# A transformer sandwich kernel: the first fillers read a constant, the last layer's scale row moves to ScalarE, and the tiles are laid out anew

## The reference, cut to what matters

```
x = x + layernorm(attention(layernorm(x)))          # 8 batches x 256 tokens x 128; softmax over 256 keys
h = silu(lin(z, w1)) * lin(z, w2)                   # z = layernorm(x); 128 -> 512
h = gelu(lin(h, h1)); h = gelu(lin(h, h2))          # 512 -> 512, exact gelu
x = x + layernorm(lin(h, w3))                       # 512 -> 128
# lin(z, w) = (z @ w.T) * s, with one scale s per output column; all in fp32
```

## Time and profile before

| what | us |
|---|---|
| time, median of 3 runs (lowest to highest) | 132.6 (132.56 to 133.0) |
| the profiled execution, its time | 133.0 |
| the profiled execution, its span from first to last instruction | 131.1 |
| PE busy in the span | 123.2 (94%) |
| DVE / ACT / POOL busy | 101.5 / 97.2 / 28.5 |

### The profile page before, as it was taken

The page is one execution under the profiler, slowest core; times in us unless marked ns, Lnnn a source line. Parts: engine busy times, 40 slices in busy tenths (PEclk is TensorE's granted clock), DMA queues, the critical chain, the costliest instruction groups (busy, mean ns, idle before and its releaser), DMA issues.

```text
span 131.1 us, 2357 instructions
## 1 busy us (share of the span) xinstructions
PE 123.2 (94%) x699; PEld 102.0 (78%) x699; DVE 101.5 (77%) x339; ACT 97.2 (74%) x180; POOL 28.5 (22%) x41
## 2 busy tenths in 40 slices
PE   5999999999899999999999999999999999999950
PEld 4677869888778888887889888888787887799940
DVE  1587898998799989838799898376989935996660
ACT  3238887986999748399999095999993996996510
POOL 5282420035300054002000463300021330000450
PEclk9999999999999999999999999999999999999999
DMA  4799996001200000000000001020000011000021
GB/s 111 246 342 387 376 388 218 1 5 14 69 0 5 0 7 0 0 0 0 5 0 0 0 5 40 0 80 10 0 0 0 0 52 33 0 5 0 5 80 43
DMA packets 5344, 8.28 MB, mean 63 GB/s; under 512 B 464, under 2 KB 2768, under 8 KB 5328
## 3 DMA queue, kind: packets, MB, share of 16 engines
q1 hardware_dynamic: 3984, 5.19, 12.0%
q0 software_dynamic: 1344, 2.88, 6.8%
HBM read 7.02 MB, written 1.05 MB: 62 GB/s over the span
## 4 chain that ended last, share of the span: by engine, by line
PE 85%; DVE 6%; DMA 2%; issue 1%; ACT 1%; POOL 1%; SPq 0%; DVEq 0%; ACTq 0%
PE F L1170 22%; PE F L1176 22%; PE F L1123 5%; PE A L1051 5%; PE F L1130 5%; PE A L1083 4%; PE A L1170 2%; PE A L1176 2%; PE A L1034 2%; PE A L1067 2%; DMA wa_raw<-w_attn 2%; PE A L1022 2%; PE A L1014 1%; PE F L1199 1%; PE A L1211 1%
## 5 line engine op out<-in xcount | busy, mean ns | idle before, releaser
L317 POOL TENSOR_TENSOR rstd<-mv,minus_half 128x4 f32<-128x4 f32 (+1 forms) x19 | 18.4, 971 | 89.3 <-DVE mv L619 89.3
L1170 PE MATMUL F<-a_hi,h_hi 128*128 128x512 f32 (+1 forms) x160 | 37.5, 356 | 0.0
L1176 PE MATMUL F<-a_lo,h_hi 128*128 128x512 f32 (+1 forms) x160 | 36.8, 350 | 0.2 <-DVE a_lo L612 0.2
L612 DVE TENSOR_TENSOR a_lo<-act_full,a_hi 128x512 fp32r<-128x512 f32 (+1 forms) x52 | 30.1, 601 | 5.2 <-ACT act_full L430 4.9
L438 ACT ACTIVATE a_hi<-F,sc 128x512 fp32r<-128x512 f32 (+1 forms) x35 | 21.1, 627 | 14.1 <-PE F L1176 13.9
L1176 PEld LDWEIGHTS F<-a_lo,h_hi 128*128 128x128 f32 x160 | 26.6, 188 | 5.1 <-DVE a_lo L612 0.8
L1170 PEld LDWEIGHTS F<-a_hi,h_hi 128*128 128x128 f32 x160 | 25.9, 188 | 4.2 <-ACT act_full L430 0.4
L430 ACT ACTIVATE act_full<-F,sc 128x512 f32<-128x512 f32 (+1 forms) x40 | 23.4, 619 | 1.6 <-PE F L1176 1.6
L715 DVE SCALAR_TENSOR_TENSOR act_full<-F,sc,silu 128x512 f32<-128x512 f32 (+1 forms) x16 | 10.7, 676 | 1.9 <-ACT silu L419 1.6
L1123 PE MATMUL F<-x2T_hi,w_hi 128*128 128x512 f32 (+1 forms) x32 | 10.3, 404 | 0.5 <-issue 0.3
L419 ACT ACTIVATE silu<-F,sc 128x512 f32<-128x512 f32 (+1 forms) x16 | 9.9, 634 | 1.0 <-PE F L1130 0.7
(11 more groups left out here) (154 smaller groups left out, 194.5 us busy)
## 6 DMA issues: line engine op xcount, KB each, us to landing
h_raw<-h SPq DMA_DIRECT2D x2, 1024.0 KB, 11.2
h_hi<-h POOLq DMA_DIRECT2D x2, 1024.0 KB, 9.2
xs<-x SPq DMA_DIRECT2D x3, 256.0 KB, 3.9
out<-outs SPq DMA_DIRECT2D x3, 256.0 KB, 2.2
w_raw<-w SPq DMA_DIRECT2D x1, 512.0 KB, 6.4
w_hi<-w POOLq DMA_DIRECT2D x1, 512.0 KB, 7.0
xs<-x SPq DMA_DIRECT2D x2, 128.0 KB, 8.7
w_raw<-w SPq DMA_DIRECT2D x1, 256.0 KB, 15.5
```

Source lines behind the costliest of these rows:

```text
L317: nc.gpsimd.tensor_tensor(rstd[:, ln, tiles(b)], mv[:, ln, tiles(b), 1], minus_half[:, 0:SIZES[b]], ALU.pow).then_inc(rstd_ready[ln], 1)
L612: nc.vector.tensor_tensor(dst, full, hi.bitcast(f32), ALU.subtract).then_inc(done, 1)
L1170: nc.tensor.matmul(out, terms[k][0], terms[k][2], start=(k == 0), stop=False)
L1176: last = [nc.tensor.matmul(out, terms[k][0], terms[k][3], start=False, stop=(k == KT - 1)) for out, terms in groups]
```

## The change

The fillers read a constant of the preamble, one bf16 value per partition, spread over 256 columns, instead of the tile `warm`; the clearing of `warm`, its semaphore and PE's wait for it are gone. The first groups of fillers become 13, 3 and 2 where they were 10, 6 and 3; the eight later ones stay. `w3_diagonal` and `w3_row_copy` move from DVE to ACT, where each is an activation of the kind Copy, between `xT_copy(0)` and `gT_copy(0)`, and between `v_copy(0)` and `exps(0, 0)`. The allocation has a new order: after `wa_raw` come three small tiles of together 384 bytes, then all the tiles whose size is a multiple of 2048 bytes, then the rest.

```diff
         wa_raw = sb("wa_raw", [P, 3 * D])
+        rstd = sb("rstd", [P, 4, TILES])
+        neg_max = sb("neg_max", [P, TILES])
+        sums = sb("sums", [P, TILES])
+
+        x2T_hi, x2T_lo = sb("x2T_hi", [P, TOK], f32r), sb("x2T_lo", [P, TOK], f32r)
+        a_hi = [sb(f"a{n}_hi", [P, KT, TOK], f32r) for n in (1, 2, 3)]
+        a_lo = [sb(f"a{n}_lo", [P, KT, TOK], f32r) for n in (1, 2, 3)]
+        act_full = sb("act_full", [P, KT, TOK])
+        silu1 = sb("silu1", [P, 2, TOK])
         w12_hi = sb("w12_hi", [P, 2 * HID], f32r)
...
-        sc = sb("sc", [P, N_SCALES])
-        qk = sb("qk", [P, D])
...
-        warm = sb("warm", [P, 512], mybir.dt.bfloat16)
...
+        warm = nc.const_aps.tensor(1.0, [P, 2 * P], mybir.dt.bfloat16)
+        qk = sb("qk", [P, D])
...
+        sc = sb("sc", [P, N_SCALES])
...
         @block.gpsimd
         def _(pool):
-            nc.gpsimd.memset(warm[:, :], 0.0).then_inc(warm_ready, 1)
             nc.gpsimd.memset(ident[:, :], 0.0).then_inc(zeroed, 1)
...
+            def w3_diagonal():
+                act.wait_ge(sc_loaded, 16)
+                act.wait_ge(ident_ready, 1)
+                nc.scalar.activation(w3_diag[:, :], ident[:, :], ACT.Copy, scale=sc[:, S_W3:S_W3 + 1]).then_inc(w3_diag_ready, 1)
+
+            def w3_row_copy():
+                act.wait_ge(w3_row_in_psum, 1)
+                nc.scalar.activation(w3_row[:, :], A[3][:, 0:D], ACT.Copy).then_inc(w3_row_ready, 1)
+
             qk_copy()
             xT_copy(0)
+            w3_diagonal()
             gT_copy(0)
             v_copy(0)
+            w3_row_copy()
             exps(0, 0)
...
-            def w3_diagonal():
-                dve.wait_ge(sc_loaded, 16)
-                dve.wait_ge(ident_ready, 1)
-                nc.vector.tensor_scalar(w3_diag[:, :], ident[:, :], sc[:, S_W3:S_W3 + 1], None, ALU.mult).then_inc(w3_diag_ready, 1)
-
-            def w3_row_copy():
-                dve.wait_ge(w3_row_in_psum, 1)
-                nc.vector.tensor_copy(w3_row[:, :], A[3][:, 0:D]).then_inc(w3_row_ready, 1)
-
             x_statistics(0)
             x_normalised(0)
-            w3_diagonal()
             x_statistics(1)
...
             squared_sums(0)
-            w3_row_copy()
             pT_copy(0, 0)
...
-                    nc.tensor.matmul(bank[:, 0:256], warm[:, 0:P], warm[:, 0:256], start=True, stop=True)
+                    nc.tensor.matmul(bank[:, 0:256], warm[:, 0:P], warm[:, :], start=True, stop=True)
...
-            pe.wait_ge(warm_ready, 1)
-            keep_warm(A[0], 10)
+            keep_warm(A[0], 13)
             qk_product()
             pe.wait_ge(ident_ready, 1)
-            keep_warm(A[0], 6)
+            keep_warm(A[0], 3)
             x_transposes(0)
-            keep_warm(A[0], 3)
+            keep_warm(A[0], 2)
             g_projection(0)
```

More of the change, by code:

```diff
@@ L60, in sem @@
             return ctx.enter_context(nc.semaphore(name))
+        LN_X, LN_O, LN_X1, LN_Y = range(4)
+        LOW_PARTS = ((0, 3), (3, 6))
         wa_raw = sb("wa_raw", [P, 3 * D])
+        rstd = sb("rstd", [P, 4, TILES])
[6 more added lines that the diff above has]
+        silu1 = sb("silu1", [P, 2, TOK])
         w12_hi = sb("w12_hi", [P, 2 * HID], f32r)
@@ L69, in sandwich_kernel @@
         w3_raw = sb("w3_raw", [P, KT * D])
-        sc = sb("sc", [P, N_SCALES])
-        qk = sb("qk", [P, D])
[L72 to L75, removed]
-        warm = sb("warm", [P, 512], mybir.dt.bfloat16)
[L77 to L80, removed]
         w3_scaled = sb("w3_scaled", [P, KT * D])
-        flags = sb("flags", [1, 2])
-        LOW_PARTS = ((0, 3), (3, 6))
         xs = sb("xs", [P, TILES, D])
@@ L90, in sandwich_kernel @@
         y_n = sb("y_n", [P, TB, D])
[L91 to L106, removed]
         yT = sb("yT", [P, TOK])
+        low_bits = sb("low_bits", [P, 2 * HID], mybir.dt.bfloat16)
         F = [bank(f"F{i}") for i in range(4)]
@@ L124, in sandwich_kernel @@
         borrowed, odd, even = Lane(), attention_buffers("odd"), attention_buffers("even")
+        low_pairs = sb("low_pairs", [P, HID], mybir.dt.bfloat16)
+        warm = nc.const_aps.tensor(1.0, [P, 2 * P], mybir.dt.bfloat16)
+        qk = sb("qk", [P, D])
+        wv = wa_raw[:, 2 * D:3 * D]
+        ident = sb("ident", [P, P])
+        ones_sq, w3_diag, w3_row = sb("ones_sq", [P, P]), sb("w3_diag", [P, D]), sb("w3_row", [P, D])
+        stats = sb("stats", [P, 4, TILES, 9])
+        mv = sb("mv", [P, 4, TILES, 2])
+        o_shift = sb("o_shift", [P, TILES])
+        y_scaled = sb("y_scaled", [P, TILES])
+        y_shift = sb("y_shift", [P, TILES])
+        sc = sb("sc", [P, N_SCALES])
+        minus_half = sb("minus_half", [P, TB])
+        ones = sb("ones", [P, 1])
+        low_sums = sb("low_sums", [P, 6])
+        flags = sb("flags", [1, 2])
         borrowed.xn = act_full[:, 1, 0:half].rearrange("p (t d) -> p t d", d=D)
@@ L160, in sandwich_kernel @@
             sem("w12_rounded"), sem("h1_rounded"), sem("h2_rounded"), sem("w3_rounded"))
-        warm_ready = sem("warm_ready")
         zeroed, ident_ready, eps_ready = sem("zeroed"), sem("ident_ready"), sem("eps_ready")
```

## The result

The changed kernel takes 131.61 us (median of 6 runs, 131.16 to 131.82), the kernel before 132.58 (median of 6 runs beside it, 132.18 to 134.55): a ratio of 0.989, interval 0.9851 to 0.9928. By these medians it is faster by 1.0 us, the small end of that interval; on two other chips it was 2.0 and 1.6 us (e9, e15). The prediction had 132.3 and took "the same" for the likeliest. The range held the time, but the step on which the prediction rested is only the first of three gains.

What follows compares the result with a forecast made beforehand. PE was taken as the bound: busy 94% of the span, 85% of the chain. Only six fillers becoming three counted, 0.25 us off the 132.6 median, all else 0: about 132.3 us, range 131.5 to 133.8.

Steps and rivals of the forecast that it cites:

- "the same": Outcome class for the whole kernel: no change beyond the 0.3% a measurement can tell; chance 0.47.
- the step on which the prediction rested: Cutting six fillers to three ahead of block 0's transposes; 0.25 us, the whole forecast gain.
- Constant instead of `warm`: PE's start: begins 0.57 us earlier, thirteen fillers end at 3.50, before the qk product's data; POOL's lost work worth 0.
- Six fillers become three: Before block 0's transposes: ACT's copy of xT up to 0.31 us earlier, by the clock's rise; 0.25 taken.
- Three fillers become two: Between transposes and g projection, which waits for ACT's copy and not the fillers; worth 0 on the path.
- `w3_row_copy` on ACT: In ACT's idle time before the exponentials; shortens DVE's work ahead of the `attend(0, 0)` copy, 0 to 0.1 us, 0 taken.
- `w3_diagonal` on ACT: Between ACT's copies of xT and g, covered by 0.1 us; DVE's freed time and earlier POOL loads worth 0.
- New addresses: Large tiles at multiples of 2048: float32r streaming could gain or lose up to 5.7 us; 0 taken.
- The small gains add up: Rival: transposes 0.31, copy ahead of `attend(0, 0)` 0.1, earlier loads up to 0.2; 131.6 to 132.2 us, chance 0.14.
- The addresses speed up float32r: Rival: 32-byte phase causes float32r's 7.5% excess, so half to all of 5.7 us goes; 127 to 130, chance 0.11.
- Nothing on the path: Rival: with an early clock rise the six fillers never stood in the way; 132.5 to 132.7 us, chance 0.12.
- The clock comes up late: Slower rival: fewer early fillers delay PE's clock, transposes to scores cost up to 2.05 us more; 133.0 to 134.5, chance 0.15.

Runs made afterwards that it cites:

- e9: The changed kernel as it is, run again on another chip: 131.42 us, ratio 0.985 to the kernel before.
- e15: The changed kernel as it is, run a third time on a further chip: 131.4 us, ratio 0.9869 to the kernel before.
- e3: The kernel before with only the constant in the fillers and the counts 13, 3, 2; old addresses, scale row on DVE: 132.55 us, ratio 0.9966.
- e7: The changed kernel with the float32r weights alone 32 bytes further on, activations left in place: 134.08 us in one execution.
- e10: The changed kernel with the old counts of the later fillers (13, 6, 3): 131.65 us, ratio 0.9868 to the kernel before.
- e14: The kernel before with filler counts 10, 3, 2, still waiting for `warm`: 132.81 us, ratio 0.9974.
- e11: The changed kernel with the float32r weights alone 64 bytes further on: 133.39 us in one execution.
- e4: The kernel before with only the scale row's two steps moved from DVE to ACT: 132.5 us, ratio 0.9952.
- e5: The changed kernel with seven added waits at the head of DVE's list, bringing it back to 448 records: 132.32 us, ratio 0.9925 to the kernel before.
- e6: The kernel before with the scale row's two steps on ACT and seven added waits at the head of DVE's list: 133.14 us, ratio 0.9991.
- e1: The changed kernel with the tiles in the old allocation order, every tile at its old address: 131.69 us, ratio 0.9887 to the kernel before.
- e8: The changed kernel with all float32r tiles, weights and activations alike, 32 bytes further on: 131.41 us in one execution.
- e2: The kernel before with the new allocation order of tiles alone: 132.77 us, ratio 0.9969.

## Why the prediction was right or wrong

**Constant instead of `warm`**: right. Thirteen fillers fit (the last starts at 3.29, the qk product at 3.69) at the price of the old ones, 0.21 us apart, and no row shows anybody waiting for POOL's lost operation. What it does to the rise of the clock the prediction counts with the next step: it took the same 3.9 us behind the first filler, so 4.6 us. That is not a fixed distance. In the three traces of the changed kernel it shifts from one execution to the next: by the spacing of the matmuls it was about 4.3 us in the first, between 5.6 and 6.1 in e9, and between 5.8 and 6.3 in e15. Over all traces it goes from 3.7 (e3) to 9.9 us (e7). The GHz that the prediction gives for the two levels are in no view; the rows show the spacings of fillers of 256 columns, 0.21 and 0.11 us.

**Six fillers become three**: right in place, 0.25 taken, 0.48 measured in the profile of the whole start, of which 0.37 lie between x and the copy. The 0.31 of the working was for transposes at the high clock; the clock rose earlier still than the 4.6 us assumed, and x came 0.11 us earlier. That the 0.48 came out so well is partly luck: against the same trace before, e9 and e15 gain 0.19 and 0.01. The steadier figure is e3's 0.45 by the times, for the constant and the counts together; that the counts do it isn't shown (e10, e14). The mean of the maxima's start is 8.33 in ten traces that start PE at 0.78, and 8.80 in five that start it at 1.32; this leaves out e7 and e11, and with their late clocks the ten become twelve with a mean of 8.62.

**Three fillers become two**, **`w3_row_copy` on ACT**: right for the path, no row shows anything of them on it. `w3_row_copy` has left DVE's list too, though, and so has its part in the next step.

**`w3_diagonal` on ACT**: right on its place and its cover (done at 6.02, load at 6.11, so 0.09 us to spare where 0.1 was forecast), and no row shows a cost of the earlier POOL loads. It is wrong in the sentence on DVE, "so this is worth 0". This is **the step that failed**. It asked only who waits for DVE's next operation, and not what else goes with the length of DVE's list. In all 17 traces that length and the tail go together: with 448 records in DVE's list (six traces) an 8-KB packet of q14 begins 1.73 to 1.78 us before the end of the span, beside the last store, and the last 16 matmuls begin 6.56 to 6.68 us before that end; with 445 (eleven) the packet begins 1.63 to 1.84 us behind it, and the matmuls 5.48 to 5.56 before it. Other lengths were not tried. e4 shows it without the rest of the change, and e5 and e6 undo it with instructions that do no work. So the term put at 0 measured 1.1 us of span. That the packet brings instructions for DVE, and comes later because DVE's list is shorter, is my reading; the traces show only that the two go together.

By the times it is smaller. e1 and e3 lie 0.86 us apart, e4 0.6 us under the kernel before, both on one chip. All runs together say why: the part of the time outside the span is 1.75 to 1.97 us in each of 130 runs with the long list, and 2.10 to 2.29 in each of 50 with the short one. Where the packet of q14 comes behind the last instruction, about 0.35 us of the 1.1 come back outside the span; that leaves 0.75. Whether it is the packet that takes this time isn't shown.

**New addresses**: bounds right (-5.7 to 5.7), the value not. What "twice through its columns" stands for in the rows is a time, 0.215 us for 256 columns of plain fp32 against 0.110 for a bf16 filler of as many. "I take 0, as every float32r tile has the same phase today" is the second step that failed: weights and activations did not have the same phase. The prediction's own figures say so: the float32r weights began at 16512 + 1536 = 18048, a multiple of 64, and the activations 32 bytes past one. That distance, not the phase, is what e7 and e8 show to count. The term measured 0.4 to 0.5 us in the body's length (e2 and the changed kernel), from 512-column matmuls 2 to 3% faster (from 234 ns to between 227 and 230) and 256-column ones 3% slower; by the times alone e2's interval just reaches no change. Those of the first layer, 231 to 234 ns by the mean of their spacing in every kernel, hardly took part. By count it should be more: 192 wide matmuls some 6 ns shorter and 128 narrow ones 2 to 3 ns longer make about 0.8 us (an estimate from these spacings). Part of it is lost again, since behind 99 us the chain of the changed kernel leaves PE:

```profile
99.96 0.69 ACT a_hi L436
...
105.80 0.94 ACT L417
...
107.60 0.49 DVE pT_odd L724
```

The chain of the kernel before stays on PE through all of this stretch. This is the 7% of ACT on the page, and e2, with the new addresses alone, has it too (7%).

The distances of 32, 64 and 256 bytes are not alike: 0.93 us at 32 and 64 against 0.91 to 0.92 at 0 and 256 for four wide ones, and 0.70 or 0.71, 0.68 and 0.72 for six narrow ones at 32, 64 and 0.

**The rivals.** *The small gains add up* has the time (131.6 to 132.2) without the reason: neither the earlier copy nor the earlier loads show on the path. *The addresses speed up float32r* was right that the addresses count, and had the wrong size: a tenth of the 5.7 us that it allowed, and it pulled the other way for narrow matmuls. *Nothing on the path* fell with e3. *The clock comes up late* is real and was priced right (2.05 us forecast; 10.38 - 8.13 = 2.25 in e7, 9.78 - 8.13 = 1.65 in e11). What sets it off stays open. e7 and e11 have PE idle before the qk product, whose data came late, but e2 has its qk product as late (4.07 against 4.12 in e7) and its clock rose at about 5.5 us, with the old six and three fillers; and e14, with three and two, had a late clock behind an early qk product. So the thinner row of fillers that the prediction named isn't ruled out: all three late clocks are among the twelve traces that have it, none among the five with the old row. None of the 17 runs of the changed kernel itself, in three groups of runs, was over 131.82, so its weight on the changed kernel is small. Runs of the kernel before reach 134.6; whether by this too isn't shown, as those were not profiled.

**What would show it**: the first filler at 0.75 (0.78), the copy near 5.5 (5.35), the maxima near 8.3 (8.13) came true. Pieces at 0.233 and "everything behind 10 us as it was" did not.

What stays open: the shares of early start and counts (e3, e10, e14 don't separate them); what brings the clock up late; why the distance of weights and activations counts, and why not in the first layer; distances between 64 and 256, which were not tried but for 192; what the packet of q14 is for; and why the time outside the span is longer when it falls there.

## What to carry to other kernels

Before an edit is costed at nothing, ask what it does to the length of its engine's list of instructions and to every address behind it: here the runs that altered these two moved the tail by 1.1 us (e4) and the body by 0.45 (e2), while no row shows a gain from the moved work itself. Look at the last store of the profile as at any other part: see whether a packet of an instruction queue lies beside it, try a list that is a few instructions shorter (three records did it here), and take the gain from the times, as part of it can come back behind the span (0.35 of 1.1 us here). And compare an expensive float32r matmul's weights and activations by the distance of their addresses, at each width that the kernel uses, before choosing an order of allocation.

## What the runs showed of the hardware

- With 448 records in DVE's list (six traces, ACT's list 284 or 287) a packet of 8192 bytes on q14, kind "instruction", begins 1.73 to 1.78 us before the end of the span, beside the last store of 64 KB, and takes 0.31 to 0.41 us. With 445 (eleven traces, ACT's list 287) it begins 1.63 to 1.84 us behind that end. The last store lands 2.65 to 2.76 us after its issue in the six, 1.62 to 1.64 in the eleven (SP's last wait 2.2 to 2.3 against 1.2).
- In e5 the packet takes 0.40 us (5.0% of 16 engines over 0.5 us), and a sixteenth of the last store's packets begin at 128.98 us, as it ends, where the others begin from 128.25 on. From 128.25 to 128.98 are 0.7 us; the remaining 0.3 lie between the last packet and the landing (0.65 us in e5, 0.35 in the changed kernel), and their cause stays open.
- Seven added waits at the head of DVE's list, fulfilled by the time x lands, delay the first operation behind them by 0.36 us (e5, e6: 0.38 us from the landing of x to the statistics, 0.02 in the other traces).
- In the two layers of 512 to 512 a float32r matmul of 512 columns took 227 to 230 ns with weights and activations 0 or 256 bytes apart, 232 to 234 at 32 and 64; one of 256 columns took 120 at 0 and 256, 117 to 118 at 32, 114 at 64 and 192 (pieces of four and six in the chain). In the first layer 231 to 234 ns at every distance.
- The granted clock reads 1.00 while matmuls run at nearly half rate (e7: a piece of 1.22 us where 0.70 is usual), so the clock of the first 10 us has to be read from the spacing.
